# A pre-sorted two-slot adapter kernel: the first batch's x no longer waits for the sort, and what starts the tensor engine is reordered

## The reference, cut to what matters

```python
h = jnp.einsum('bsh,bhk->bsk', hidden_states, W_down[role]) + b_down[role][:, None, :]
h = jax.nn.gelu(h, approximate=False)
u = jnp.einsum('bsk,bkh->bsh', h, W_up[role]) + b_up[role][:, None, :]
y = hidden_states + u
mean = jnp.mean(y, axis=-1, keepdims=True)
var = jnp.mean(jnp.square(y - mean), axis=-1, keepdims=True)
yn = (y - mean) * jax.lax.rsqrt(var + LN_EPS)
return yn * gamma[role][:, None, :] + beta[role][:, None, :]
```

## Time and profile before

| what | us |
|---|---|
| median of 3 runs | 1417.38 (1417.31 to 1417.69) |
| the profiled execution's own time | 1416.96 |
| its span, first to last instruction | 1415.2 |
| TensorE busy in it | 1401.1 |

### The profile page before, as it was taken

How to read it: one execution, slowest core, us unless ns; L and a number is a source line. 1 busy time by engine, 2 the same in 40 slices (tenths; PEclk the granted TensorE clock), 3 DMA queues, 4 the chain that set the end, 5 groups by cost and what they waited for, 6 DMA issues and landing times.

```text
span 1415.2 us, 29331 instructions
## 1 busy us (share of the span) xinstructions
PE 1401.1 (99%) x6175; PEld 1158.2 (82%) x6176; DVE 1204.8 (85%) x1458; ACT 776.8 (55%) x2047; POOL 201.0 (14%) x300
## 2 busy tenths in 40 slices
PE   8999999999999999999999999999999999999997
PEld 6888888888888888888888888888888888888886
DVE  8798988888888888888888899988888888888887
ACT  5555555555555555555555555555555555555555
POOL 4376311100000000000000377311100000000000
PEclk9999999999999999999999999999999999999999
DMA  8677777766566666665666778777765666656654
GB/s 230 183 225 241 215 212 200 211 195 198 184 195 199 194 184 196 200 192 184 194 200 193 213 227 234 222 198 201 218 199 185 196 200 190 185 194 199 192 186 149
DMA packets 208868, 283.49 MB, mean 200 GB/s; under 512 B 25791, under 2 KB 155584, under 8 KB 208846
## 3 DMA queue, kind: packets, MB, share of 16 engines
q1 hardware_dynamic: 201438, 269.34, 61.4%
q0 software_dynamic: 5888, 12.07, 4.6%
q10 hardware_dynamic: 1520, 1.84, 0.4%
HBM read 183.27 MB, written 99.88 MB: 200 GB/s over the span
## 4 chain that ended last, share of the span: by engine, by line
PE 98%; DVE 1%; DMA 1%; issue 0%; ACT 0%; DVEq 0%; ACTq 0%
PE p_up L1120 16%; PE p_up L1118 16%; PE p_up L1119 16%; PE p_down L1118 16%; PE p_down L1120 16%; PE p_down L1119 16%; DMA row<-in_L_cond_W_down 0%; DMA x_quad<-in_x 0%; DVE row L1038 0%; PE p_hT L1114 0%; DVE row L866 0%; DMA w_raw<-in_itok_B 0%; DVE x_quad L820 0%; DVE wd_lo L758 0%; DVE x_quad L1024 0%
## 5 line engine op out<-in xcount | busy, mean ns | idle before, releaser
L1118 PE MATMUL p_down<-wd_hi,xT_hi 128*128 x1012 | 393.9, 389 | 0.7 <-DVE xT_lo L782 0.4
L1120 PE MATMUL p_down<-wd_hi,xT_lo 128*128 x1012 | 393.7, 389 | 0.0
L1119 PE MATMUL p_down<-wd_lo,xT_hi 128*128 x1012 | 393.7, 389 | 0.0
L1118 PE MATMUL p_up<-wu_hi,hT_hi 128*128 x1008 | 392.3, 389 | 0.0
L1120 PE MATMUL p_up<-wu_hi,hT_lo 128*128 x1008 | 392.1, 389 | 0.0
L1119 PE MATMUL p_up<-wu_lo,hT_hi 128*128 x1008 | 392.1, 389 | 0.0
L595 ACT ACTIVATE hT_hi<-p_hT 128x512 fp32r<-128x512 f32 x126 | 75.7, 601 | 381.5 <-DVE p_hT L800 378.9
L820 DVE SCALAR_TENSOR_TENSOR row<-p_up,row 128x1024 f32<-128x1024 f32 x126 | 154.2, 1224 | 126.3 <-PE p_up L1120 126.2
L581 ACT ACTIVATE xT_hi<-xT_raw 128x1024 fp32r<-128x1024 f32 x125 | 132.8, 1062 | 187.6 <-PE p_down L1120 185.6
L1118 PEld LDWEIGHTS p_down<-wd_hi,xT_hi 128*128 128x128 f32 x1012 | 189.6, 187 | 40.8 <-issue 1.4
L1119 PEld LDWEIGHTS p_down<-wd_lo,xT_hi 128*128 128x128 f32 x1012 | 190.3, 188 | 39.7
(11 more groups left out here) (174 smaller groups left out, 981.3 us busy)
## 6 DMA issues: line engine op xcount, KB each, us to landing
x_quad<-in_x SPq DMA_DIRECT2D x510, 128.0 KB, 3.4
row<-in_x SPq DMA_DIRECT2D x126, 512.0 KB, 4.0
out<-row SPq DMA_DIRECT2D x126, 512.0 KB, 2.7
h_dram<-h SPq DMA_DIRECT2D x125, 256.0 KB, 4.1
h_quad<-h_dram SPq DMA_DIRECT2D x498, 64.0 KB, 1.9
w_raw<-in_L_cond_W_down POOLq DMA_DIRECT2D x64, 64.0 KB, 3.2
w_raw<-in_L_cond_W_up POOLq DMA_DIRECT2D x64, 64.0 KB, 3.6
row<-in_L_cond_W_up SPq DMA_DIRECT2D x16, 128.0 KB, 3.6
```

Source lines behind the costliest of these rows:

```text
L1118: pe.matmul(dst, a_hi, w_hi, start=first, stop=False)
L1119: pe.matmul(dst, a_hi, w_lo, start=False, stop=False)
L1120: return pe.matmul(dst, a_lo, w_hi, start=False, stop=last)
```

## The change

- x of batch 0 is loaded at once, by SyncE and ScalarE, before roles are known. The role of batch 0 is read into a register on both and picks the W pieces (`role_of_first`); that role comes first in the order.
- The keys are computed on all 128 partitions (roles are broadcast by the DMA), so the two matmuls that spread them go; the full sort (`sort_all`) moves behind the start's splits, its matmul behind batch 1's product.
- Bias, gamma and beta rows of all three roles are loaded: by SyncE, ScalarE and, for three of the eight DMAs, GpSimd. Their rounding moves from VectorE to ScalarE. The selector picks the role's rows.
- Each x half and each W piece of batches 1 and the later pieces are issued half by SyncE after `first_known`, half by ScalarE between its activations.
- TensorE starts with 18 and then 10 fillers of 256 columns on a constant, then takes the first product in three passes (high by high, low by high, high by low), with the spreads between its matmuls and the down bias of batch 0 added by one more spread into its accumulator.

```diff
-    PAIRED = LOW + NROWS
+    PAIRED = LOW + R * NROWS
+    FILL = 2 * P
+        def role_of_first(eng):
+            eng.wait_ge(roles_loaded, 16)
+            return eng.value_load(role_row[0:1, 0:1], min_val=0, max_val=R - 1)
+        def load_x0(eng, quads):
+            for q in quads:
+                src = x_view[0:1, q].rearrange("o t g f -> (o t) g f")
+                eng.dma_start(x_quad[0][BLK * q:BLK * q + BLK, :, :], src).then_inc(quad_loaded[0], 16)
+        def load_param_rows(eng, src, at, loaded):
+            eng.dma_start(h[at:at + src.shape[0], 0:512], src).then_inc(loaded, 16)
...
         @block.sync
-            sp.dma_start(role_row, role.rearrange("(o b) -> o b", o=1)).then_inc(roles_loaded, 16)
+            sp.dma_start(role_row, role.partition_broadcast(P)).then_inc(roles_loaded, 16)
+            load_x0(sp, range(0, NQ // 2))
             sp.wait_ge(param_rows_clear, 1)
+            load_param_rows(sp, beta_rows, BETA_ROW, param_rows_loaded)
+            load_param_rows(sp, beta_rows, LOW + BETA_ROW, param_rows_loaded)
+            first_role = role_of_first(sp)
+            for n in range(2):
+                load_first(sp, first_role, n, range(0, NQ // 2))
...
+            load_quads(sp, numbers[1], 1, range(0, NQ // 2))
+            for n in range(2, FD):
+                load_first(sp, first_role, n, range(0, NQ // 2))
+            sp.wait_ge(x_transposed, 1)
+            load_quads(sp, numbers[2], 0)
...
         @block.gpsimd
+            pool.memset(wu_lo[:, 0:FILL].bitcast(F32), 1.0).then_inc(filler_ready, 1)
...
+            pool.wait_ge(param_rows_clear, 1)
+            load_param_rows(pool, gamma_rows, LOW + GAMMA_ROW, more_rows_loaded)
+            load_param_rows(pool, up_bias_rows, UP_BIAS_ROW, more_rows_loaded)
+            load_param_rows(pool, up_bias_rows, LOW + UP_BIAS_ROW, more_rows_loaded)
...
         @block.vector
             params_at, when_loaded = [], []
-            dve.wait_ge(param_rows_loaded, 16 * 8)
-            dve.tensor_copy(rows, rows_raw).then_inc(param_rows_hi, 1)
+            transpose_half(0, 0)
+            pick_rows()
+            transpose_half(0, 1)
             dve.wait_ge(param_rows_hi, 1)
             dve.tensor_tensor(rows[LOW:PAIRED, :], ...)
+            subtract_half(0, 0)
             split_first(0)
+            transpose_half(1, 0)
+            split_chunk(1, 0, chunk_split)
+            split_chunk(1, 1, first_split)
+            subtract_half(0, 1)
+            subtract_half(1, 0)
+            split_first(2)
+            transpose_half(1, 1)
+            split_first(3)
+            subtract_half(1, 1)
+            sort_all()
+            transpose_half(2, 0)
+            transpose_half(2, 1)
+            subtract_half(2, 0)
...
         @block.tensor
+            pe.wait_ge(filler_ready, 1)
+            keep_clock(18)
+            pe.wait_ge(first_known, 2)
+            pe.load(weights_reg, first_slots[0:1, 0:RING])
+            keep_clock(10)
+            def first_product():
+                pe.wait_ge(half_hi, 1)
+                pe.wait_ge(first_hi, 1)
+                hi_by_hi(*args, range(0, 2))
+                pe.wait_ge(ident_ready, 2)
+                pe.wait_ge(param_rows_split, 1)
+                spread(p_hT[:, :], 0).then_inc(params_spread, 1)
+                spread(p_up[1][:, 0:512], 1)
+                spread(p_up[1][:, 512:H], 2).then_inc(params_spread, 1)
+                pe.wait_ge(half_lo, 1)
+                lo_by_hi(*args, range(0, 2))
+                spread(p_sq[:, 0:512], 3)
+                spread(p_sq[:, 512:H], 4).then_inc(params_spread, 1)
+                pe.wait_ge(first_split, 1)
+                hi_by_lo(*args, range(0, 2))
+                pe.wait_ge(first_hi, 2)
+                hi_by_hi(*args, range(2, 4))
+                lo_by_hi(*args, range(2, 4))
+                spread(p_up[0][:, 0:512], 5)
+                spread(p_up[0][:, 512:H], 6).then_inc(params_spread, 1)
+                spread(p_down[:, :], 0, False)
+                pe.wait_ge(chunk_split, 1)
+                hi_by_lo(*args, range(2, 3))
+                pe.wait_ge(first_split, 2)
+                return hi_by_lo(*args, range(3, 4))
...
+            first_product().then_inc(half_down, 1)
             half_product(1, 0, other, weights_at[1]).then_inc(half_down, 1)
-            half_product(0, 1, p_down[:, :], weights_at[0]).then_inc(down_done, 1)
+            second_product().then_inc(down_done, 1)
             half_product(1, 1, other, weights_at[1]).then_inc(down_done, 1)
+            pe.matmul(p_up[0][0:1, 2 * B:3 * B], number_col[:, :], onehot, start=True, stop=True).then_inc(order_in_psum, 1)
             turn_h(0)
```

More of the change, by code:

```diff
@@ L120, in adapter_kernel @@
         table = sb("table", [1, NUMBER + B + 8], I32)
-        ones_row, ident = h_quad[0:1, 0, :], h_quad[:, 1, :]
+        index_row, ident, onehot, key = h_quad[:, 0, :].bitcast(I32), *(h_quad[:, n, :] for n in range(1, 4))
         first_keys = sb("first_keys", [1, 8], I32)
@@ L545, in _ @@
         def _(act):
-            load_first(act, 0, range(0, 1))
+            load_x0(act, range(NQ // 2, NQ - 1))
             act.wait_ge(out_ready, 1)
             act.activation(factor[:, 0:1], opener[:, 2:3], ACT.Gelu)
-            load_first(act, 0, range(1, NQ))
-            load_first(act, 1)
+            load_x0(act, range(NQ - 1, NQ))
+            act.wait_ge(param_rows_clear, 1)
+            load_param_rows(act, b_down, 0, param_rows_loaded)
+            load_param_rows(act, b_down, LOW, param_rows_loaded)
+            load_param_rows(act, gamma_rows, GAMMA_ROW, param_rows_loaded)
+            first_role = role_of_first(act)
+            for n in range(2):
+                load_first(act, first_role, n, range(NQ // 2, NQ))
+            number_reg = [act.alloc_register(f"first_number{n}") for n in range(RING)]
             act.wait_ge(first_known, 1)
-            load_quads(act, act.value_load(first_numbers[0:1, 0:1], min_val=0, max_val=B - 1), 0, range(NQ // 2, NQ))
+            act.load(number_reg, first_numbers[0:1, 0:RING])
+            numbers = [act.snap(reg, min_val=0, max_val=B - 1) for reg in number_reg]
             def round_first(n):
@@ L1156, in body, with hi_by_hi @@
                     mm.then_inc(up_done, 1)
-            def half_product(b, half, dst, at):
-                hi, lo = half_x(b, half)
-                for c in range(half * HALF, half * HALF + HALF):
-                    if (b, c) == (0, FC // K):
-                        pe.wait_ge(chunk_split, 1)
-                    elif (b, c) == (0, FC // K + 1):
-                        pe.wait_ge(first_split, 2)
-                    elif b == 0 and c % (FC // K) == 0:
-                        pe.wait_ge(first_split, c // (FC // K) + 1)
-                    mm = product(dst, hi[:, c % HALF, :], lo[:, c % HALF, :], cols(wd_hi, at + c * K, K),
-                                 cols(wd_lo, at + c * K, K), c == 0, c == HC - 1)
-                return mm
+            def hi_by_hi(b, half, dst, at, chunks):
+                hi, _ = half_x(b, half)
+                for c in chunks:
+                    pe.matmul(dst, hi[:, c % HALF, :], cols(wd_hi, at + c * K, K), start=c == 0, stop=False)
@@ new lines, in hi_by_lo, with lo_by_hi @@
+            def hi_by_lo(b, half, dst, at, chunks):
+                hi, _ = half_x(b, half)
+                for c in chunks:
+                    mm = pe.matmul(dst, hi[:, c % HALF, :], cols(wd_lo, at + c * K, K), start=False, stop=c == HC - 1)
+                return mm
+            def lo_by_hi(b, half, dst, at, chunks):
+                _, lo = half_x(b, half)
+                for c in chunks:
+                    mm = pe.matmul(dst, lo[:, c % HALF, :], cols(wd_hi, at + c * K, K), start=False, stop=False)
+                return mm
@@ new lines, in half_product @@
+            def half_product(b, half, dst, at):
+                chunks = range(half * HALF, half * HALF + HALF)
+                pe.wait_ge(half_hi if half == 0 else x_hi_ready, b + 1)
+                hi_by_hi(b, half, dst, at, chunks)
+                pe.wait_ge(half_lo if half == 0 else x_lo_ready, b + 1)
+                lo_by_hi(b, half, dst, at, chunks)
+                return hi_by_lo(b, half, dst, at, chunks)
+            def first_product():
+                at = weights_at[0]
+                args = 0, 0, p_down[:, :], at
+                pe.wait_ge(half_hi, 1)
[22 more added lines that the diff above has]
+                return hi_by_lo(*args, range(3, 4))
@@ new lines, in second_product @@
+            def second_product():
+                at = weights_at[0]
+                args = 0, 1, p_down[:, :], at
+                pe.wait_ge(x_hi_ready, 1)
+                pe.wait_ge(first_hi, 3)
+                hi_by_hi(*args, range(4, 6))
+                pe.wait_ge(x_lo_ready, 1)
+                lo_by_hi(*args, range(4, 6))
+                pe.wait_ge(first_split, 3)
+                hi_by_lo(*args, range(4, 6))
```

(5 more changed lines are left out.)

243 lines of the change are left out of this document (110 added, 133 removed).

## The result

| | before | changed kernel |
|---|---|---|
| median of the runs, us | 1417.35 (1417.18 to 1417.69, 6) | 1422.95 (1422.08 to 1424.96, 6) |
| ratio, 95% interval | | 1.0042 (1.0029 to 1.0054) |
| profiled execution, us | 1416.96 | 1424.96 |
| its span, us | 1415.2 | 1423.2 |

The change costs 5.6 us, 0.4%, where no measurable difference was forecast (1416.7). The profiled execution is the longest of the six, so its losses are larger than the median's.

A forecast was written before the change was run, and what follows sets the result against it. TensorE, busy 1401.1 of 1415.2 us, bounds the kernel; only its start can shrink. 12.0 + 3.2 + 0.2 + 1.84 + 5.52 + 0.3 puts the mark at 23.1, 0.65 earlier: 1416.3, plus 0.42 is 1416.7 us; range 1414.6 to 1418.6.

The forecast's parts named there:

- rival 2: In the start, GpSimd's parameter rows land late, at worst 8.9, making the kernel slower: 1418.8 us; chance 0.15.
- rival 3: TensorE's clock falls back between fillers and first product: 1417.0 us, at the far end 1419.9; chance 0.08.
- On SyncE 0.86 + 0.36 … gives 3.5 for its first: SyncE's issue of W_down piece 0: first quarter at 3.5, second at 4.0, so the first product starts at 8.95.
- Pieces 2 and 3 have their last quarters issued at about 9 and 12.7: W_down in the start: 4.67 us transfers land at 13.7 and 17.4, just in time, costing nothing.
- Batch 1's x: issued 7.9, 4.1 us to land: Fourth quarter, issued by ScalarE, lands at 12.0; its low part reaches TensorE at 15.4, wanted at 14.5.
- The eight spreads and the sort's matmul on the path, 1.84 + 0.3: Work now between TensorE's useful matmuls in the start: 8 x 0.23 = 1.84 us, plus 0.3 at most.
- The fillers: TensorE's start: 18 from 1.3 to 5.2, ten from about 6 to 7.2 or 8; product starts at full clock.
- Rival 4: The start isn't shorter, as full DMA engines bring 3.1 MB until piece 3, at 15.6 before: 1417.4 us; chance 0.12.
- the mark: TensorE's transposes of batch 0's h, ending the start: at 23.75 before, forecast at 23.1, 0.65 us earlier.
- No loss behind the mark: From `turn_h` on both kernels do the same work; a mark moving without the end would show an unseen loss.

The follow-up runs named there:

- b4: The control with e4's issues by SyncE, the broadcast of the roles kept, and 52 and 5 fillers: 1418.80 us, ratio 1.0010.
- b3: The control with the roles spread by a matmul, e4's issues by SyncE, 28 fillers ahead of batch 0's choice and none behind: 1416.77 us, ratio 0.9994.
- e5: The control with SyncE holding batch 2's x and W_up until piece 3 of W_down has landed: 1420.54 us, ratio 1.0022.
- e4: Also e4_sync_issues: the control with SyncE issuing all quarters of batch 1's x and pieces 2 and 3, before batch 2's x and W_up: 1418.94 us.
- b1: The control with e6's roles by matmul and e4's issues by SyncE, 28 fillers ahead of batch 0's choice and 17 behind: 1417.72 us, ratio 1.0003.
- e3: The control with 34 more fillers ahead of the choice of batch 0 and 7 more behind it: 1422.09 us, ratio 1.0034.
- the control: The changed kernel with constant waits in the start and loaded wait values kept at 16 or 1 at least: 1422.22 us, ratio 1.0034.
- e1: The control with SyncE and ScalarE issuing batch 0's x only once the roles have landed: 1423.29 us, ratio 1.0041.
- e2: The control with a four byte DMA of its own, ahead of the broadcast, feeding the role register: 1424.20 us, ratio 1.0050.
- e8: The same kernel as e6 once more, for a second profile: 1422.99 us in one execution.
- c0: Another name of the control, the changed kernel with bounded and constant waits: 1422.22 us, ratio 1.0034.
- e6: The control with the roles loaded to one partition and spread over 128 by one matmul: 1422.31 us, ratio 1.0033.

## Why the prediction was wrong, point by point

1422.95 lies above every sum of the prediction: above the forecast, the range's end of 1418.6, rival 2's 1418.8 and rival 3's 1419.9. Slower by over 0.2% had 0.05, and one of its two reasons was an error of sum: that bound is 1420.2, which rival 3's far end doesn't reach.

- *"On SyncE 0.86 + 0.36 … gives 3.5 for its first" quarter of W_down.* **This term was mis-sized by 2.3 us.** It let the roles land within the time of the issues around them, as before; they landed 3.99 behind their issue. The layout, 128 partitions, was the change's visible point, and the prediction priced no transfer for it. Worth 2.0 us (b4 against b3); the product came at 11.16, not 8.95.
- *"Pieces 2 and 3 have their last quarters issued at about 9 and 12.7 (behind batch 1's rounding); with 4.67 they land at 13.7 and 17.4 … Both cost nothing".* **This is the step that failed, and the larger one.** Piece 3's was issued at 15.91, took 6.37, landed at 22.28 instead of 17.4 and was rounded at 23.36. The order of the list was seen, its sum wasn't: the issue stands behind an activation that waits for batch 1's x, which was 3.0 late (15.0 against 12.0). And 4.67 was read from a quarter of piece 2 that was issued at 10.91, before SyncE turned to batch 2's x at 13.95; here all of batch 2's x and four quarters of W_up had been issued ahead of it from the other queue, and the hold of e5 gave 2.50. Of the two it is this transfer that cost: in e5 the issue at 14.82 made no pause. Worth 3.3 us (e4).
- *Batch 1's x: issued 7.9, 4.1 us to land.* 9.56 and 5.45. Issued by SyncE, in b4, the last piece of it took 3.40.
- *The eight spreads and the sort's matmul on the path, 1.84 + 0.3.* Right. Without a wait 56 x 0.23 + 0.3 = 13.2 was forecast, and b1, whose TensorE has no pause there, takes 13.28 (10.57 to 23.85). With the wait for batch 1's x, 8.95 to 23.1 was 14.15, and b3 takes 14.2.
- *The fillers, "ten more from about 6 to 7.2 or 8. I take it that the product starts at full clock".* Wrong: VectorE's choice came at 7.96, TensorE had waited 3.65 us, and the clock was 0.50 until 15.00. That is rival 3. The Trainium skill, "TensorE: Matmul & The Clock Gate", HAM oscillation, says that waits for a DMA between bursts of matmuls put the clock back to half rate. The trace agrees, for a wait of 3.65 us that was for VectorE (0.50 behind it). But its price in the start was 0.1 us (e3, and b4 against e4_sync_issues), since the data were later still. Where the fall did cost was after the second pause, 23.50: twelve matmuls from 25.28 took 4.5 us there and 2.8 in e4 (from 21.74 to 24.55).
- *Rival 2, GpSimd's rows.* Didn't occur. ScalarE's first activation came at 8.56, later than the 7.5 that was named as its sign, but released by `first_slots`: its sign was there, with another cause, the register load ahead of it in ScalarE's program. The landing times were read from GpSimd's own DMAs, so that the 0.4 us added to them for its path were counted twice; and here these rows took 3.9 to 4.3 us to land instead of 3.2, which puts the third near 7.3, still ahead of VectorE's choice at 7.96.
- *Rival 4, "should piece 3's last quarter take over 5 us, the mark is that of before".* The right mechanism, with 0.12; it stopped at the mark of before, as it did not ask what a later issue would add to the longer transfer. Its 15.6, the time at which piece 3 is there in the kernel before, is by the chain that of a quarter of piece 2.
- *No loss behind the mark.* 1.7 of 8.0 us in the profiled execution arose behind it, 0.8 of them in the tail; in the control, 0.6 of 4.5. In b3 the reverse shows, which the prediction had named as a sign of a loss that it hadn't seen: its mark is 0.42 earlier than that of before, but its last matmul starts at 1406.68 against 1406.72, and both spans are 1415.2. In b1 the mark is 0.10 later and the last matmul (1406.89) 0.17. No experiment took these apart; they stay open.

## What to carry to other kernels

When a DMA moves to the end of a queue that issues between waiting activations, its start follows all the waits ahead of it; write those out before taking its duration, and take that duration from a stretch in which the same other traffic is under way. A transfer that is needed next should be issued ahead of, and by the queue of, the traffic that is needed later. And a small load whose shape changes, from one partition to 128, is a new transfer with a price of its own, above all if a register, a sort and an issue hang on it.

## What the runs showed of the hardware that I had not expected

- 512 bytes of roles on one partition: 1.26 us. The same 512 bytes read for each of 128 partitions: 2.90 us with no x beside it (e1), 3.66 (e2) to 4.06 (e5) beside batch 0's x. A matmul against ones spread them in 0.8 us (from 2.54 in e8's TensorE).
- A 128 KB quarter of W_down: 5.5 to 7.3 us (e1 and e3 the least, e2 the most) with batch 2's x and W_up under way from the other queue, 2.2 and 2.5 with them held.
- The clock in the start: 1.00 granted after a pause of 0.82 (c0, e6), 0.50 after pauses of 1.64 (the changed kernel), 2.11 (e2), 2.46 (e8) and 3.65. It needn't fall in the pause: in e8 the first two matmuls behind it took 0.73 us, as at full clock, and the four from 24.92 took 1.91; in e2 the first two already took 1.21. The pauses in between, and what else decides, weren't tried.
- The granted clock of a window doesn't tell all: in e6 ten fillers took 2.50 us, as at half clock, and in e8 the same ten 1.45, while the windows over both read 1.00. Read the durations too. From e6:

```profile
7.45 2.50 PE L1147 MATMUL p_down<-wu_lo 128*128 128x256 f32 x10 [0.79 <-DVE first_slots L811]
8.00:9.00 1.00, 1.00 (x7) 1.00 (x6) 0.97 (x2) 1.00 (x2) 0.80 (x3) 1.00 0.90 265
```
